# The order of work on the last tiles of a linear-attention block: statistics, masks, residual sums and transposes

## The chip, the cores and the metric

The kernel runs on one core of a Trainium2 chip. The metric is the device time of one execution in microseconds. Before the change the median of three runs is 949.95 us (949.16 to 952.21). One further execution, with the hardware profiler on, took 948.85 us; its span from the first to the last instruction is 947.1 us, and all times of single instructions below are counted from the start of that span.

The engines are PE (matrix products and transposes; PEld is its weight load), DVE (vector), ACT (scalar), POOL (GpSimd) and SP, whose queue issues every transfer of this kernel. Each works through its own list of instructions in order; the lists meet only at semaphores.

## The reference

Two pre-norm layers on x of 8 x 1024 tokens and 512 channels, in float32:

```
x = x + attn(layernorm(x))
x = x + ffn(layernorm(x))

attn(x):  q, k, v = split(x @ W_attn + b_attn)        # 16 heads of 32
          q, k = elu(q) + 1, elu(k) + 1
          for each token t:  kv += k_t v_t^T;  ksum += k_t       # causal
                             y_t = (q_t kv) / (q_t ksum + 1e-6)
          return y @ W_proj + b_proj
ffn(x):   x8 = clip(x, -448, 448).astype(float8_e4m3)
          w8 = clip(w, -448, 448).astype(float8_e4m3)
          return x8 @ w8.T + bias
```

## The kernel before

The 8192 tokens are 64 tiles of 128 (`NT` = 64), eight tiles to a sequence. Every engine has one hand-written loop over `n`, and the order of the calls in that loop is the order of its instructions. In pass `n` the loops work on several tiles at once:

- **PE** (L433 to L470): `ahead` (parts of the q, k, v projection of later tiles; in passes 59 to 62 only the v part of tile n+1, twelve 128x512 matmuls), `t_y(n-1)` (passes 61 on: y of the tile before is transposed on PE, four 128x128), `values(n)` (64 small matmuls: masked scores and state times v), `proj(n-1)` (twelve 128x512 matmuls; y and W_proj stand as high and low float16 halves, so matmuls 0 to 7 need the transposed high half `s_yth`, and 8 to 11 the low half `s_ytl`), `update(n+1)` (the tile's k-v products), `scores(n+1)`, and `ffn(n-2)` (four 128x512).
- **DVE** (L981 to L1022): `ahead` (here `v_out(n+1)`, two operations at L728), `t_y(n-1)` (low half of the transposed y, L779), `values(n)` (division; the result is `y`), `proj(n-1)` (residual sum of the attention, L786), `ln2(n-1)` (second layernorm's statistics, L700 to L705), `update(n+1)` (`mid` and `state`, L751 and L754), `scores(n+1)` (the causal masks, two operations at L739) and `ffn(n-2)` (the last residual sum of a tile, L844, which signals `s_res`).
- **ACT** (L655 to L693): in passes 61 to 63 `t_y(n-1)` (high half of the transposed y, L610), `ffn(n-3)` (the FFN's result from PSUM, `o16`); in passes 60 to 63 `t2(n-2)` (the normed row to float8 and to bfloat16, `x2b`), `k_tokens(n+1)` (`ktok`, which `update` on PE reads), `queries(n+1)`, and `spread(n+1)` (state and mid into the operand of `values`).
- **POOL** (L1159 to L1189): `k_split(n+2)`, `proj(n-1)` (inverse square root at L1029 and the norm at L1031, which gives `x2`), `spread(n+1)` (a part of mid, `s_near`, at L1052), `add_bf(n-1)` (L1095).
- **SP** (L1265 to L1298), in pass n: transpose `x2t` of tile n-2 (L1234, read by PE's `ffn(n-2)`), transpose of the k bytes of tile n+2 (L1222), then the store of tile n-2. In the code the pass ends so:

```
t2(n - 2)
t_k(n + 2)
sp.wait_ge(s_res, m + 1)            # m = n - 2
e.dma_start(out_d[m * P:(m + 1) * P, :], xs[:, m % NX, :])
```

So `x2t` of tile m+1 is issued behind the store of tile m, and that store waits for `s_res` of tile m, the residual sum of DVE's `ffn(m)`. This part is in both kernels the same. `tail(n)` is true from tile 60 on: from there y goes through PE's transposes and not through a transfer, and `update` and `scores` of the next tile stand ahead of `ffn` on PE. PSUM banks are taken in turn from a ring of four (`take`).

From pass 60 on DVE's `ffn(58)` stands at the end of pass 60, `ffn(59)` of 61, `ffn(60)` of 62, and `ffn(61)`, `ffn(62)` and the last tile's in pass 64. On PE, pass 63 is `t_y(62)`, `proj(62)` matmuls 0 to 3, `values(63)`, `proj(62)` 4 to 11, `t_y(63)`; pass 64 projects tile 63 in two halves of 256 columns (`last_proj`), then `ffn(61)`, the transposes of tiles 62 and 63, and their FFN.

Of the kernel before, what the change touches and what calls it, by code (L numbers as in the profile page):

```python
# [21 lines left out]
NT = B * T // P  # L22
# [28 lines left out]
def tail(n):  # L51
    return n >= NT - 4
# [31 lines left out]
def build(nc, x_d, wa_d, ba_d, wp_d, bp_d, wf_d, bf_d, out_d):  # L84
    ctx = ExitStack()
    with ctx:
# [133 lines left out]
        def _(e):  # L220
# [3 lines left out]
            def take(key, freed, value):  # L224

                r = ring["n"] % NR
                ring["n"] += 1
                if ring["free"][r]:
                    pe.wait_ge(*ring["free"][r])
                ring["free"][r] = (freed, value)  # L230
                bank[key] = R[r]
                return R[r]
# [4 lines left out]
            def transposes(out, ins):  # L237
                for i, a in enumerate(ins):
                    last = e.transpose(out[:, i * P:(i + 1) * P], a, ident[:, :])  # L239
                return last  # L240
# [112 lines left out]
            def t_y(n):  # L353
                out = take(("ty", n), s_ytl, n - NT + 5)
                pe.wait_ge(s_y, n + 1)
                transposes(out, [y[:, h * P:(h + 1) * P] for h in range(4)]).then_inc(s_ty, 1)

            def proj(n, first=0, end=12):
                out = take(("proj", n), s_x1, n + 1) if first == 0 else bank["proj", n]
                pe.wait_ge(s_wpl, 1)  # L360
                if tail(n):
                    pe.wait_ge(s_yth, n - NT + 5)
                else:
                    pe.wait_ge(s_yt[n % 2], 16 * (n // 2 + 1))
                mms = [(a + h, b, h) for a, b in ((0, wph), (0, wpl), (4, wph)) for h in range(4)]
                for i, (k, b, h) in list(enumerate(mms))[first:end]:
                    if tail(n) and i == 8:
                        pe.wait_ge(s_ytl, n - NT + 5)
                    mm = matmul(out[:, :], yt[:, n % 2, k, :], b[:, h, :], i == 0, i == 11)
                if end == 12:  # L370
                    mm.then_inc(s_proj, 1)
# [61 lines left out]
            for n in range(NT + 2):  # L433
                if n < NT:
                    if not tail(n):
                        scores(n)
                    ahead(chunks(n)[0])
                    if tail(n - 1):
                        t_y(n - 1)
                    if n:  # L440
                        ahead(chunks(n)[1])
                    if n == NT - 1:

                        proj(n - 1, 0, 4)
                    values(n)
                    if n == 0:
                        ahead(chunks(n)[1])
                if n == NT - 1:
                    proj(n - 1, 4, 12)
                    t_y(n)  # L450
                elif n == NT:
                    last_proj()
                elif 1 <= n < NT:
                    proj(n - 1)
                if n + 1 < NT and tail(n + 1):

                    update(n + 1)
                    scores(n + 1)
                if n == NT:
                    ffn(n - 3)  # L460
                    t2(n - 2)
                    pe.wait_ge(s_y, NT)
                    warm(8)
                    last_t2()
                    ffn(n - 2)
                    last_ffn()
                elif 2 <= n < NT - 1:
                    ffn(n - 2)
                if n + 1 < NT and not tail(n + 1):
                    update(n + 1)  # L470
# [225 lines left out]
        def _(e):  # L696
# [35 lines left out]
            def scores(n):  # L732
                dve.wait_ge(s_score, n + 1)
                dve.wait_ge(s_causal, 3)
                if n:
                    dve.wait_ge(s_av, n)
                for a in range(2):
                    dst = sm[half_rows(a), :, a, :].rearrange("p h (g t) -> p h g t", g=4)
                    made = e.tensor_tensor(dst, scored(a), causal_over(a), ALU.mult)  # L739
                made.then_inc(s_smd, 1)  # L740
# [36 lines left out]
            def t_y(n):  # L777
                dve.wait_ge(s_yth, n - NT + 5)
                e.tensor_tensor(yt[:, n % 2, 4:8, :], four(bank["ty", n][:, :]), yt[:, n % 2, 0:4, :],  # L779
                                ALU.subtract).then_inc(s_ytl, 1)  # L780
# [200 lines left out]
            for n in range(NT + 2):  # L981
                if n < NT:
                    if not tail(n):
                        scores(n)
                    if n + 8 < NT:
                        ln1(n + 8)
                    if n == 0:
                        proj_weight()
                    if n == 1:
                        ffn_sum(0, 2)  # L990
                    ahead(chunks(n)[0])
                    if tail(n - 1):
                        t_y(n - 1)
                    if n:
                        ahead(chunks(n)[1])
                    values(n)
                    if n == 0:
                        ffn_high()
                        ffn_round()
                        ahead(chunks(n)[1])  # L1000
                if 1 <= n < NT:
                    proj(n - 1)
                if n == NT - 1:
                    t_y(n)
                if 1 <= n < NT:
                    ln2(n - 1)
                if n == NT:
                    last_proj()
                if n + 1 < NT:
                    update(n + 1)  # L1010
                    if tail(n + 1):
                        scores(n + 1)
                if n == 1:
                    ffn_sum(2, 4)
                if n == NT:
                    last_norm()
                    ffn(n - 3)
                    last_t2()
                    ffn(n - 2)
                    last_ffn()  # L1020
                elif 2 <= n < NT - 1:
                    ffn(n - 2)  # L1022

        @block.gpsimd
        def _(e):
# [16 lines left out]
            def spread(n):  # L1042

                v = v1[:, n % NV, :, :, :].rearrange("p a (g h) w -> p a g h w", g=4)
                pool.wait_ge(s_pair, 3)
                pool.wait_ge(s_one, 2)
                if n >= NV:
                    pool.wait_ge(s_av, n - NV + 1)
                pool.wait_ge(s_mid, n + 1)
                held = mid[0:HALF, :].rearrange("p (g w) -> p g w", g=4).unsqueeze(2).broadcast_to([HALF, 4, 2, W])  # L1050
                rows = pair[:, :].unsqueeze(1).unsqueeze(3).broadcast_to([HALF, 4, 2, W])
                e.tensor_tensor(v[0:HALF, 1, :, 0:2, :], held, rows, ALU.mult).then_inc(s_near, 1)  # L1052
# [19 lines left out]
            def add_bp(m):  # L1072
                x = xs[:, m % NX, :]
                pool.wait_ge(s_xn, m + 1)
                pool.wait_ge(s_bias, 32)
                e.tensor_tensor(x, x, bp[:, :], ALU.add).then_inc(s_xb, 1)  # L1076
# [8 lines left out]
            def proj(n):  # L1085
                x = xs[:, n % NX, :]
                pool.wait_ge(s_var2, n + 1)
                if n >= 2:
                    pool.wait_ge(s_x28, n - 1)
                norm(x2[:, n % 2, :], x, st2[:, n % 4, :], s_rs2, s_x2, n)  # L1090
# [68 lines left out]
            for n in range(NT + 1):  # L1159
                if n < NT:  # L1160
                    if n + 8 < NT:
                        ln1(n + 8)
                    if n == 0:
                        values(n)
                    elif n + 8 < NT:
                        add_bp(n + 8)

                    if n % 4 == 3 and n + 8 < NT:
                        ln1_parts(n + 8)
                    if n + 2 < NT:  # L1170
                        k_split(n + 2)
                    if n % 4 < 3 and n + 8 < NT:
                        ln1_parts(n + 8)
                    if n:
                        values(n)
                    if 1 <= n < 8:
                        add_bp(n)
                if n == NT:
                    last_norm()
                    last_ffn()  # L1180
                elif n >= 1:
                    proj(n - 1)
                if n + 1 < NT:
                    spread(n + 1)
                if n == 0:
                    add_bp(n + 8)
                    add_bp(n)
                if 1 <= n < NT:
                    add_bf(n - 1)  # L1189
# [134 lines left out]
```

## Time and profile before

| | before |
|---|---|
| median of the runs | 949.95 us |
| profiled execution | 948.85 us |
| its span | 947.1 us |
| PE busy | 918.2 us, 97% of the span |
| DVE / ACT / POOL busy | 731.8 / 745.6 / 641.3 us |
| transfers issued by SP | 251840 packets, 96.25 MB |

A timeline row gives the start, the length, the engine, the line, the operation with its output and inputs, the shapes and the count; in brackets the idle time of the engine just before it and what ended it. Matmuls are pipelined and their ends are modelled, so a row of PE may be longer than the distance to the next one. A few matmul records are missing from a trace: a row `x3` of `wft,x2t` is an FFN of four.

### The profile page before, as it was taken

How to read it: one execution, taken by the hardware profiler on the slowest of the kernel's cores; microseconds unless marked ns; L12 is line 12 of the kernel's file. 1: busy time of each engine (PE TensorE's matmuls, PEld its weight loads, DVE VectorE, ACT ScalarE, POOL GpSimd, SP SyncE). 2: the span in 40 equal slices, each digit the busy share in tenths (PEclk: the TensorE clock that was granted, in tenths of full speed). 3: DMA queues.
4: the chain of work that ended last, by engine and by line, in shares of the span. 5: the costliest groups of instructions: out<-in, count | busy, mean ns of one | idle time of the engine just before them, and what ended most of it. 6: DMA issues, size and time to landing. Idle time of an engine off the chain costs nothing.

```text
span 947.1 us, 44776 instructions
## 1 busy us (share of the span) xinstructions
PE 918.2 (97%) x19470; PEld 490.5 (52%) x19532; DVE 731.8 (77%) x1404; ACT 745.6 (79%) x1358; POOL 641.3 (68%) x713
## 2 busy tenths in 40 slices
PE   5998999999999999999999999999999999999896
PEld 2455555555555555555555555555555555555454
DVE  6999879787777777778687687777778687676687
ACT  5788787877869688787877868788787878868874
POOL 5659877766767677676776667677676676764433
PEclk9999999999999999999999999999999999999999
DMA  8926564565464554565555465555555455462421
GB/s 268 143 41 109 109 119 103 97 119 97 95 122 100 98 116 104 96 114 105 95 114 107 91 116 106 89 118 108 92 114 112 89 114 110 90 103 59 76 69 59
DMA packets 252036, 99.12 MB, mean 105 GB/s; under 512 B 232384, under 2 KB 232640, under 8 KB 251840
## 3 DMA queue, kind: packets, MB, share of 16 engines
q1 hardware_dynamic: 251840, 96.25, 52.3%
q8 instruction: 154, 2.52, 1.1%
q14 instruction: 42, 0.34, 0.1%
HBM read 22.81 MB, written 16.78 MB: 42 GB/s over the span
## 4 chain that ended last, share of the span: by engine, by line
PE 90%; POOL 3%; issue 2%; ACT 2%; DVE 2%; SPq 1%; DMA 1%; ACTq 0%; POOLq 0%
PE R L235 77%; PE S L235 13%; POOL st L1029 1%; POOL xn L1031 1%; DMA x2t<-x2b 0%; ACT raw L477 0%; POOL xs L1076 0%; PE R L239 0%; DVE raw L739 0%; POOL raw L1062 0%; DMA xs<-in_L_attn_x 0%; ACT ktok L477 0%; SPq L1227 0%; DVE v L728 0%; ACT o L477 0%
## 5 line engine op out<-in xcount | busy, mean ns | idle before, releaser
L235 PE MATMUL R<-xt,wh 128*128 128x512 f16 x1024 | 306.2, 381 | 2.4 <-ACT wh L477 2.4
L716 DVE SCALAR_TENSOR_TENSOR qk<-qk,rel 128x512 f32<-128x512 f32 x128 | 112.8, 884 | 118.1 <-ACT rel L489 118.1
L477 ACT ACTIVATE raw<-qk 64x512 f32<-64x512 f32 x256 | 160.8, 628 | 48.9 <-PE S L235 45.7
L235 PE MATMUL R<-xt,wl 128*128 128x512 f16 x512 | 194.0, 380 | 0.0
L1083 POOL TENSOR_TENSOR yhl<-y,yhl 128x512 f16<-128x512 f32 x60 | 70.0, 1167 | 146.1 <-ACT yhl L477 146.1
L235 PE MATMUL R<-wh,xt 128*128 128x512 f16 x512 | 158.0, 379 | 0.0
L235 PEld LDWEIGHTS R<-xt,wh 128*128 128x128 f16 x1024 | 96.7, 98 | 116.0 <-DVE xt L882 2.6
L739 DVE TENSOR_TENSOR raw<-S,causal 64x1024 f32<-64x1024 f32 x128 | 155.9, 1218 | 0.9
L1029 POOL TENSOR_TENSOR st<-st,half 128x1 f32<-128x1 f32 x127 | 92.7, 730 | 90.6 <-DVE st L705 89.8
L235 PE MATMUL R<-wph,yt 128*128 128x512 f16 (+1 forms) x520 | 132.4, 377 | 3.9 <-ACT yt L477 1.9
L486 ACT ACTIVATE qk<-R,bqk,wm 128x512 f32<-128x512 f32 x128 | 98.9, 773 | 35.6 <-PE R L235 35.0
L728 DVE SCALAR_TENSOR_TENSOR v<-R,wm,bv 64x512 f32<-64x512 f32 x128 | 96.0, 750 | 8.2 <-PE R L235 5.7
L1062 POOL COPY raw<-qk 128x512 int16<-128x512 int16 x126 | 86.8, 717 | 21.2 <-DVE qk L716 14.9
L489 ACT ACTIVATE rel<-R,bqk,wm 128x512 f32<-128x512 f32 x128 | 98.5, 769 | 3.0 <-DVE qk L716 3.0
L235 PE MATMUL R<-wl,xt 128*128 128x512 f16 x256 | 97.0, 379 | 0.0
L700 DVE BATCH_NORM_STATS2 st<-xs 128x6 f32<-128x512 f32 x127 | 88.2, 694 | 6.4 <-DMA xs<-in_L_attn_x 2.5
L235 PEld LDWEIGHTS S<-v,raw 128*32 128x32 f32 x8192 | 76.2, 108 | 29.3 <-issue 27.1
L477 ACT ACTIVATE ktok<-raw 128x512 int16<-128x512 int16 x126 | 88.2, 771 | 0.1
L1076 POOL TENSOR_TENSOR xs<-xs,bp 128x512 f32<-128x512 f32 x64 | 84.6, 1322 | 4.6
L235 PE MATMUL S<-v,raw 128*32 128x33 f32 x8192 | 83.5, 198 | 2.5 <-issue 1.9
L1069 POOL TENSOR_TENSOR xnhl<-xn,xnhl 128x512 f16<-128x512 f32 x60 | 69.6, 1161 | 23.7 <-ACT xnhl L477 23.7
L477 ACT ACTIVATE v<-state 32x132 f32<-32x132 f32 x256 | 79.9, 312 | 3.8
(108 smaller groups left out, 1364.8 us busy)
## 6 DMA issues: line engine op xcount, KB each, us to landing
xs<-in_L_attn_x SPq DMA_DIRECT2D x64, 256.0 KB, 3.1
out<-xs SPq DMA_DIRECT2D x63, 256.0 KB, 2.4
raw<-in_L_attn_W_attn SPq DMA_DIRECT2D x3, 1024.0 KB, 9.5
xs<-in_L_attn_W_proj SPq DMA_DIRECT2D x4, 256.0 KB
raw<-in_L_ffn_weight SPq DMA_DIRECT2D x1, 1024.0 KB, 17.0
raw<-raw SPq DMA_TRANSPOSE x63, 3.7
x2t<-x2b SPq DMA_TRANSPOSE x62, 2.5
xt<-xnhl SPq DMA_TRANSPOSE x60, 3.5
```

What stands on the lines that cost most here:

```text
L235: return e.matmul(out, a, b, start=start, stop=stop, skip_group_check=True)
L477: return e.activation(out, in_, ACT.Copy, **more)
L486: e.activation(dst[:, i, :], bank["qkv", j, i][:, :], ACT.Exp, scale=UN[i // 4], bias=bqk[:, i:i + 1])
L489: e.activation(rel[:, u % 2, :], bank["qkv", j, i][:, :], ACT.Relu, scale=UN[i // 4], bias=bqk[:, i:i + 1]).then_inc(s_relu, 1)
L700: e.bn_stats(row[:, 0:6], src).then_inc(s_bn, 1)
L716: e.scalar_tensor_tensor(qk[j % 2][:, i, :], qk[j % 2][:, i, :], 1.0, rel[:, (u - 1) % 2, :], ALU.min, ALU.add).then_inc(s_phi, 1)
L728: made = e.scalar_tensor_tensor(v1[rows, n % NV, a, :, 0:32], heads(bank["qkv", j, 8 + t][rows, :]), UN_V[rows], heads(bv[rows, :]), ALU.m ...
L739: made = e.tensor_tensor(dst, scored(a), causal_over(a), ALU.mult)
L1029: e.tensor_tensor(row[:, 10:11], row[:, 9:10], half[:, :], ALU.pow).then_inc(s_rs, 1)
L1062: made = e.tensor_copy(khl[:, n % 2, w, :].rearrange("p (g t) -> p g t", g=4), words[:, w, :, :])
L1076: e.tensor_tensor(x, x, bp[:, :], ALU.add).then_inc(s_xb, 1)
L1083: e.tensor_tensor(yhl[:, n % 2, 1, :], y[:, :], yhl[:, n % 2, 0, :], ALU.subtract).then_inc(s_yl, 1)
```

## The change

Only the order of calls in four loops changes, for the passes 59 to 64; no operation is added or taken away, and SP's and ACT's lists stay as they are.

- **DVE**, passes 59 to 62: `update(n+1)` and the masks stand ahead of `ln2(n-1)`. `ffn` of a tile from 58 on comes later: `ffn(58)` at the end of pass 61, not 60; `ffn(59)` of pass 62, not 61; `ffn(60)` in pass 63 between the residual sum of tile 62 and `t_y(63)`. Pass 60 has no `ffn`.
- **POOL**, passes 59 to 62: `spread(n+1)` ahead of `proj(n-1)`.
- **PE**: `ffn(60)` moves from the end of pass 62 to pass 63, between `t_y(62)` and `values(63)`; `proj(62)` runs whole behind `values(63)`, with `t_y(63)` between its matmuls 0 to 7 and 8 to 11.

```
 PE     if n == NT - 1:
-           proj(n - 1, 0, 4)
+           ffn(n - 3)
        values(n)
    if n == NT - 1:
-       proj(n - 1, 4, 12)
+       proj(n - 1, 0, 8)
        t_y(n)
+       proj(n - 1, 8, 12)
...
-   elif 2 <= n < NT - 1:
+   elif 2 <= n < NT - 2:
        ffn(n - 2)
 DVE    if n == NT - 1:
+           ffn(n - 3)
            t_y(n)
+       if n + 1 < NT and tail(n + 1):
+           update(n + 1)
+           scores(n + 1)
        if 1 <= n < NT:
            ln2(n - 1)
...
-       if n + 1 < NT:
+       if n + 1 < NT and not tail(n + 1):
            update(n + 1)
-           if tail(n + 1):
-               scores(n + 1)
...
-       elif 2 <= n < NT - 1:
+       elif n < NT - 1 and tail(n - 1):
+           ffn(n - 3)
+       elif n >= 2 and not tail(n):
            ffn(n - 2)
 POOL
+       if n + 1 < NT and tail(n + 1):
+           spread(n + 1)
...
            proj(n - 1)
-       if n + 1 < NT:
+       if n + 1 < NT and not tail(n + 1):
            spread(n + 1)
```

DVE's list in pass 61 before, from the residual sum of tile 60 (`xs<-R1`) over its statistics (`st2`), `mid` and `state` of tile 62 and its masks (`raw`) to the last residual sum of tile 59 (`xs<-o16`), the v of tile 63 and the low half of y of tile 61 (`yt`):

```order
L786 SCALAR_TENSOR_TENSOR xs<-R1,wm,xs 128x512
L700 BN_STATS st2<-xs 128x6
L702 BN_AGGR st2<-st2 128x2
L704 TENSOR_SCALAR st2<-st2 128x1
L705 TENSOR_SCALAR st2<-st2 128x1
L751 TENSOR_TENSOR mid<-R2,state 128x132
L754 TENSOR_TENSOR state<-R3,mid 128x132
L739 TENSOR_TENSOR raw<-S,causal 64x4x256 x2
L844 TENSOR_TENSOR xs<-o16,xs 128x512
L728 SCALAR_TENSOR_TENSOR v1<-R1,wm,bv 64x16x32 x2
L779 TENSOR_TENSOR yt<-R2,yt 128x512
```

The statistics stand four operations earlier here than in the changed list, in which the sum is that of tile 58 (line numbers are one higher):

```order
L787 SCALAR_TENSOR_TENSOR xs<-R1,wm,xs 128x512
L752 TENSOR_TENSOR mid<-R2,state 128x132
L755 TENSOR_TENSOR state<-R3,mid 128x132
L740 TENSOR_TENSOR raw<-S,causal 64x4x256 x2
L701 BN_STATS st2<-xs 128x6
L703 BN_AGGR st2<-st2 128x2
L705 TENSOR_SCALAR st2<-st2 128x1
L706 TENSOR_SCALAR st2<-st2 128x1
L845 TENSOR_TENSOR xs<-o16,xs 128x512
L729 SCALAR_TENSOR_TENSOR v1<-R1,wm,bv 64x16x32 x2
L780 TENSOR_TENSOR yt<-R2,yt 128x512
```

The masks moved ahead of the statistics, and the row `xs<-o16` stays in its place but belongs to a tile one older.

PE's list from behind the scores of tile 63 to the projection of tile 62, as one piece of the difference (`wft,x2t` is the FFN of tile 60, `ident,y` the transposes of y of tile 62 and then 63, `wph` and `wpl` the projection of tile 62, `v1,raw` the values of tile 63):

```order
-L235 MATMUL R1<-wft,x2t 128x512 x4
-L239 MATMUL R2<-ident,y 128x128 x4
-L235 MATMUL R3<-wph,yt 128x512 x4
-L235 MATMUL S<-v1,raw 32x33 x64
+L239 MATMUL R1<-ident,y 128x128 x4
+L235 MATMUL R2<-wft,x2t 128x512 x4
+L235 MATMUL S<-v1,raw 32x33 x64
+L235 MATMUL R3<-wph,yt 128x512 x4
 L235 MATMUL R3<-wpl,yt 128x512 x4
-L235 MATMUL R3<-wph,yt 128x512 x4
 L239 MATMUL R0<-ident,y 128x128 x4
+L235 MATMUL R3<-wph,yt 128x512 x4
```

The FFN of tile 60 moved behind the transposes and stays ahead of the values; four matmuls of the projection moved behind the values, and its last four behind the transposes of tile 63.

## Rows read from the trace of the kernel before

**Rows 1.** Page, part 4: the chain that ended last, shares by engine

```profile
PE 90%; POOL 3%; issue 2%; ACT 2%; DVE 2%; SPq 1%; DMA 1%; ACTq 0%; POOLq 0%
```

**Rows 2.** Timeline of PE in passes 60 to 63

```profile
903.61 0.76 PE L235 MATMUL R<-v,ktok 64*32 64x33 f32 x64
...
913.45 1.04 PE L235 MATMUL R<-wph,yt 128*128 128x512 f16 x4 [1.12 <-DVE yt L779]
...
915.11 0.91 PE L235 MATMUL S<-qk 32*64 32x64 f32 x64
916.18 0.81 PE L235 MATMUL R<-wft,x2t 128*128 128x512 bf16 x3 [0.16 <-issue]
916.83 0.38 PE L235 MATMUL R<-wh,xt 128*128 128x512 f16 x1
...
922.34 0.60 PE L235 MATMUL R<-wph,yt 128*128 128x512 f16 x2 [0.56 <-issue]
...
924.19 1.04 PE L235 MATMUL R<-wph,yt 128*128 128x512 f16 x4 [0.38 <-DVE yt L779]
...
927.26 0.60 PE L239 MATMUL R<-ident,y 128*128 128x128 f32 x4
929.04 1.02 PE L235 MATMUL R<-wph,yt 128*128 128x512 f16 x4 [1.18 <-ACT yt L477]
929.99 1.30 PE L235 MATMUL S<-v,raw 128*32 128x33 f32 x128
```

**Rows 3.** Timeline of SP's queue: stores (L1298) and transposes of x2 (L1234)

```profile
901.56 0.33 SPq L1298 DMA_DIRECT2D out<-xs  x1
901.98 1.38 SPq L1234 DMA_TRANSPOSE x2t<-x2b  x1
...
911.15 0.33 SPq L1298 DMA_DIRECT2D out<-xs  x1
911.73 1.19 SPq L1234 DMA_TRANSPOSE x2t<-x2b  x1
```

**Rows 4.** Timeline of ACT in pass 60: x2b of tile 58, k of tile 61

```profile
898.80 0.63 ACT L477 ACTIVATE x2b<-x 128x512 bf16<-128x512 fp8e4 x1
899.34 1.43 ACT L477 ACTIVATE ktok<-raw 128x512 int16<-128x512 int16 x2
```

**Rows 5.** Timeline of DVE: statistics, masks, last residual sums, low half of y

```profile
895.41 0.69 DVE L700 BATCH_NORM_STATS2 st<-xs 128x6 f32<-128x512 f32 x1
...
897.08 2.45 DVE L739 TENSOR_TENSOR raw<-S,causal 64x1024 f32<-64x1024 f32 x2
899.55 1.98 DVE L844 TENSOR_TENSOR xs<-o,xs 128x512 f32<-128x512 f16 x1
...
910.42 0.70 DVE L844 TENSOR_TENSOR xs<-o,xs 128x512 f32<-128x512 f16 x1 [1.31 <-ACT o L477]
...
934.75 0.69 DVE L779 TENSOR_TENSOR yt<-R,yt 128x512 f16<-128x512 f32 x1 [0.84 <-ACT yt L477]
```

**Rows 6.** Waits of SP's queue, 880 to 947 us: in total, times, longest

```profile
SPq L1298 <- DVE xs L844: 36.8, 7, 8.0
```

**Rows 7.** Tile x2t, 880 to 947 us: time from issue to landing

```profile
DMA to landing us min/median/max: 2.4/2.7/2.9
```

**Rows 8.** Timeline of POOL in pass 59: the norm of tile 58

```profile
896.65 0.55 POOL L1029 TENSOR_TENSOR st<-st,half 128x1 f32<-128x1 f32 x1 [0.19 <-DVE st L705]
897.30 0.77 POOL L1031 TENSOR_SCALAR x<-xs,st 128x512 f32<-128x512 f32 x1
```

**Rows 9.** Windows at the end: busy us (count) by engine, then granted clock, DMA

```profile
943.50:945.40 1.90, 0.00 (x0) 0.00 (x0) 1.11 (x3) 0.11 (x1) 0.67 (x1) 0.98 0.45 164
945.40:947.10 1.70, 0.00 (x0) 0.00 (x0) 0.00 (x0) 0.00 (x0) 0.00 (x0) 0.50 0.38 125
```

**Rows 10.** Timeline of PE: the first 128x512 matmuls of the kernel

```profile
16.13 3.57 PE L235 MATMUL R<-xt,wh 128*128 128x512 f16 x8 [2.37 <-ACT wh L477]
19.49 1.45 PE L235 MATMUL R<-xt,wl 128*128 128x512 f16 x4
```

## The prediction

> **What bounds the kernel now.** I read the chain of work that ended last first: PE carries 90% of the span [rows 1]. So a change in the last passes counts only by what PE waits for there and by the chain from the last tile's y to the last store. The timeline of PE is next. Up to pass 59 the change leaves everything alone; in passes 61 to 63 PE stands still four times [rows 2]: 1.12 us for the low half of y of tile 60, 0.56 us with no releaser shown, 0.38 us for the low half of tile 61 and 1.18 us for the high half of tile 62, together 3.24 us. These are what a new order could win.
>
> The view that decides, I think, is another one, the timeline of SP's queue. It does not alternate freely: a store of a finished tile, then, 0.4 to 0.6 us behind it, the transpose `x2t` of the next tile [rows 3]. The row of pass 60 shows that the transpose waits for the store and not for its own data: ACT had written `x2b` of tile 58 at 898.80 + 0.63 = 899.43 [rows 4], yet its transpose was issued at 901.98, 0.42 us behind the store of tile 57 at 901.56 [rows 3], and that store went out 0.03 us after DVE's residual sum of tile 57 ended, at 899.55 + 1.98 = 901.53 [rows 5]. The queue's own waits say it in sum: stores waited for the residual sum seven times in the last 67 us, 36.8 us together [rows 6]. So the residual sum of tile m holds the transpose of tile m+1, and that transpose feeds PE's FFN of tile m+1. Before, this costs nothing: the store of tile 58 goes at 911.15, the transpose of tile 59 at 911.73 [rows 3], it lands 2.7 us later [rows 7], at 914.4, and PE comes to that FFN only at 916.18 [rows 2], 1.8 us later.
>
> **The change part by part.**
>
> *Masks ahead of statistics, `near` ahead of the norm.* DVE's statistics of tile 58 began at 895.41 and were with POOL at 896.65 [rows 5, 8], so 1.2 us; now they begin behind the masks (2.45 us, rows 5) and the state, about 3.3 us later than before. The norm on POOL (896.65 to 898.07, rows 8) and ACT's `t2` go with them, and ACT is in order: its k of tile 61, ready at 899.34 + 1.43 = 900.77 [rows 4], is ready at 904.1. PE began to use it at 903.61 [rows 2]: a new wait of 0.5 us. In return `values` gets its masks somewhat sooner, which is cover only, since PE comes to `values(60)` no earlier. In passes 60 to 62 ACT had more room and I take 0.
>
> *Residual sums later.* In pass 61 DVE no longer waits 1.31 us for ACT's FFN copy [rows 5] ahead of `v_out` and the low half of y, so PE's 1.12 us go [rows 2]. With the 0.5 us of above, and the few tenths by which PE's rows overlap, the scores of tile 62 end at 915.1 in place of 915.11 + 0.91 = 916.0: -0.9 us.
>
> But the sum of tile 58 now stands at the end of pass 61, behind masks of tile 62 and statistics of tile 60. From the end of those scores: 0.1 + masks 2.45 + statistics 1.2 + sum 0.70 [rows 5] = 4.45 us, so 919.55. Then the store, 0.42 us on the queue, the transpose of tile 59 at 920.0, landing 2.7 us later [rows 3, 7]: 922.7. PE's next work, unchanged, is exactly the FFN of tile 59. **It waits 915.1 to 922.7, 7.6 us**, and starts 6.6 us later than at 916.18. Queued behind it on PE are v of tile 63 and all the rest, so nothing else fills the hole.
>
> The same once more for tile 60. Before, PE needed from 916.18 to 927.86 (929.04 less 1.18, rows 2) for that FFN, v of tile 63, the transposes of tile 61, values, projection, update and scores, the FFN of tile 60 and the transposes of tile 62: 11.7 us, less the 0.56 and 0.38 us that should not return, less 0.87 us for the FFN of tile 60: 9.9 us. So PE is ready for the FFN of tile 60 at 922.7 + 9.9 = 932.6, the scores of tile 63 having ended 0.5 us before. DVE then does the masks of tile 63, the statistics of tile 61 and only then the sum of tile 59: 932.1 + 4.45 = 936.5; store and transpose 0.4 us, landing 2.7 us: 939.6. **PE waits 7.0 us**, because this FFN was put ahead of `values(63)`; before, it was behind nothing late. `values(63)` starts at 939.6 + 0.9 = 940.5 and not at 929.99: +10.5 us.
>
> *PE's transposes of tile 63 inside the projection of tile 62.* These save the 1.18 us wait (already in the sum) and let y of tile 63 go out as soon as it is there. But the last four matmuls of tile 62 now end later, so its residual sum on DVE too, and behind that stand the sum of tile 60 and then the low half of tile 63, on which the last projection waits. From the start of `values(63)`: `values` up to 1.30, eight matmuls at 0.22, four transposes up to 0.60, four matmuls up to 1.04 [rows 2], 4.7 us less the overlap of the rows, 4.6 us; then three DVE operations of 0.7 us each (0.70 and 0.69, rows 5) = 6.7 us. Before it was 934.75 + 0.69 - 929.99 = 5.45 us. So **+1.3 us** on the final chain; from there on (statistics, norm, transposes, FFN, store) the order is the same, and the late transpose of tile 61 (behind the sum of tile 60) lands beside DVE's work on tile 63.
>
> Sum: 10.5 + 1.3 = **+11.8 us**. For the profiled execution that is 948.85 + 11.8 = 960.65; against the median, which lies 1.1 us higher, 949.95 + 11.8 = 961.75.
>
> *The clock after a stall.* Two holes of 7 us in PE are something the trace of before does not have in the middle. At its end it has one: PE was idle from 943.5 on, and from about 945.4 the granted clock is 0.50, the 1.2 GHz level [rows 9]. And its start shows what work costs at that level (the matmuls of the start follow 2.37 us of idle): eight 128x512 in 16.13 to 19.49, 0.42 us each, four more in up to 1.45 us [rows 10], against 0.22 us each later (three in 916.18 to 916.83, rows 2); the twelve cost up to 2.2 us too much before the pace doubled, 2.0 us if the last row's overlap is left out. So a price per restart between 0 (the clock stays) and 3.4 us (I allow half as much again and more, as one start says little of the spread); I take 2.0 us for the first restart, where 12 matmuls of that shape follow, and 1.7 us for the second, where `values` with its small matmuls may not be slowed: +3.7 us.
>
> The Trainium skill says in TensorE: Matmul & The Clock Gate, Part 1, that "the default state is throttled, and activity releases the throttle", and in its section Why this matters for your kernels that idle gaps between bursts of matmuls bring half clock back. By that rule both restarts are slow (965.4 us); without it the sum stays at 961.7 us. The end of the trace agrees with it (0.50 two microseconds after the last matmul), and no row shows a long hole in the middle.
>
> Forecast: 949.95 + 11.8 + 3.7 = **965.4 us**, slower by 1.6%.
>
> **The rivals.**
>
> *Stalls without the clock's part.* The holes come, and PE returns at 2.4 GHz. For: the trace has no restart in the middle, and where DVE is late anyway a slow PE is hidden. Against it the fall at the end [rows 9], after a shorter hole. 961.7 us; down to 960.5 if the masks or the landing are quicker than I take them (2.4 us is the fastest landing, rows 7).
>
> *One hole only.* If ACT or DVE slip so that the second transpose meets a PE that is late anyway, only the first hole and the tail count: 949.95 - 0.9 + 7.6 - 1.3 + 1.3 = 956.7. Against: after the first hole PE, DVE and SP stand in the same order to one another as before it.
>
> *The other side: not slower, the change does what it says.* It needs the transposes not to be held by the stores, that is SP going past a store that waits. Then the 3.24 us of waits go, 0.5 us come for k, 1.3 us for the tail, and about 1 us because PE comes to `values(63)` before its masks are done: 949.95 - 0.4 = 949.5, within 0.3%. It decides from the point where the transpose of tile 59 lands before 915.1, that is where its store goes out before 912. Against it: the 2.55 us that a ready `x2b` of tile 58 stood behind a store [rows 3, 4]. If in addition none of these new waits came, it would be 946.7 us.
>
> **How the numbers follow.** Forecast (both holes, slow restarts) 0.64; both holes without the clock 0.24; one hole 0.04, and 0.01 for something much slower; no hole, 949.5 us, 0.05; all gains, 946.7 us, 0.02. About 0.3%, 2.85 us, is what a measurement of this kernel can tell from no change. Slower by more than that: 0.64 + 0.24 + 0.04 + 0.01 = 0.93; within: 0.05; faster: 0.02. The range: from 960.5 (no clock cost, quick landing) to 968.5 (961.7 and 3.4 us at each restart).
>
> **What would show it.** In the profile after: a store of tile 58 near 919.6 and the transpose of tile 59 at once behind it; PE's first `wft,x2t` row of pass 61 with some 7.6 us idle before it and a transfer of `x2t` as releaser; the same once more, near 7 us, ahead of the FFN of tile 60; matmuls 128x512 about 0.42 us apart behind each hole and a granted clock under 1 there; ahead of the update of tile 61 a wait of some 0.5 us for ACT; no more 1.12 us ahead of the low half of tile 60's projection; 1 to 1.5 us of idle ahead of the last group of `last_proj`. The prediction is wrong if the stores of tiles 58 and 59 go out as early as before, or if PE's holes are there but the end is not later by their sum.

## The result and the profile after

The changed kernel takes 966.32 us in the median of four runs (966.21 to 966.43), against 950.70 us for the kernel before in the same rounds: ratio 1.0163, 95% interval 1.015 to 1.0175. The forecast was 965.4 us with a range of 960.5 to 968.5, so the time lies 0.9 us above the forecast and inside the range. The forecast counted from 949.95 us; by what the change adds, 15.5 us were forecast and 15.6 us came.

| | before | after |
|---|---|---|
| median of the runs | 950.70 us | 966.32 us |
| profiled execution | 948.85 us | 966.43 us |
| its span | 947.1 us | 964.7 us |
| PE busy | 918.2 us | 922.0 us |

The chain of work that ended last, shares by engine, in the page of the changed kernel (the row that answers to [rows 1]):

```profile
PE 86%; DVE 4%; POOL 3%; issue 2%; ACT 2%; DMA 1%; SPq 1%; POOLq 0%; DVEq 0%
```

PE has lost four points of the chain, DVE has gained two. PE's timeline of passes 60 to 63 shows where (the columns are those of [rows 2]):

```profile
897.19 0.76 PE L235 MATMUL R<-v,ktok 64*32 64x33 f32 x64
...
907.37 0.75 PE L235 MATMUL R<-v,ktok 64*32 64x33 f32 x64 [1.00 <-ACT ktok L478]
...
917.65 0.91 PE L235 MATMUL S<-qk 32*64 32x64 f32 x64
926.18 1.49 PE L235 MATMUL R<-wft,x2t 128*128 128x512 bf16 x3 [7.62 <-DMA x2t<-x2b]
...
936.24 0.91 PE L235 MATMUL S<-qk 32*64 32x64 f32 x64
937.08 0.66 PE L239 MATMUL R<-ident,y 128*128 128x128 f32 x4
944.81 1.49 PE L235 MATMUL R<-wft,x2t 128*128 128x512 bf16 x3 [7.07 <-DMA x2t<-x2b]
946.23 1.69 PE L235 MATMUL S<-v,raw 128*32 128x33 f32 x128
...
953.10 1.05 PE L235 MATMUL R<-wph,yt 128*128 128x256 f16 x8 [1.17 <-DVE yt L780]
```

The two holes are there, ahead of the FFN of tile 59 and ahead of that of tile 60, both ended by a transpose of x2: 7.62 and 7.07 us by these rows. But a row `x3` lacks the record of one matmul, and the FFN's weight loads show that it is the first one:

```profile
925.77 0.13 PEld L235 LDWEIGHTS R<-wft,x2t 128*128 128x128 bf16 x2 [7.35 <-DMA x2t<-x2b]
...
944.40 0.13 PEld L235 LDWEIGHTS R<-wft,x2t 128*128 128x128 bf16 x2 [6.90 <-DMA x2t<-x2b]
```

So PE stood still from 917.65 + 0.91 = 918.56 to 925.77 and from 937.08 + 0.66 = 937.74 to 944.40: 7.2 and 6.7 us. The waits of 1.12 us for the low half of tile 60 and of 1.18 us for the high half of tile 62 [rows 2] are gone. A wait of 1.00 us for k of tile 61 has come, and one of 1.17 us in the last projection.

SP's queue tells what held the transposes (stores are L1306, transposes of x2 L1242), beside ACT's writing of k of tile 61 and of `x2b` of tile 59:

```profile
905.86 1.20 SPq L1242 DMA_TRANSPOSE x2t<-x2b  x1
...
922.88 0.34 SPq L1306 DMA_DIRECT2D out<-xs  x1
923.31 1.23 SPq L1242 DMA_TRANSPOSE x2t<-x2b  x1
...
941.46 0.34 SPq L1306 DMA_DIRECT2D out<-xs  x1
941.89 1.22 SPq L1242 DMA_TRANSPOSE x2t<-x2b  x1
```

```profile
905.74 1.38 ACT L478 ACTIVATE ktok<-raw 128x512 int16<-128x512 int16 x2
...
914.90 0.63 ACT L478 ACTIVATE x2b<-x 128x512 bf16<-128x512 fp8e4 x1
```

`x2b` of tile 59 was written at 914.90 + 0.63 = 915.53, and its transpose was issued at 923.31, 7.8 us later and 0.43 us behind the store of tile 58. DVE's timeline shows what that store waited for, the residual sum (L845) behind the masks (L740) and the statistics (L701), and further down the sum of tile 60 ahead of the low half of y of tile 63 (L780):

```profile
902.55 0.68 DVE L845 TENSOR_TENSOR xs<-o,xs 128x512 f32<-128x512 f16 x1
...
918.60 2.46 DVE L740 TENSOR_TENSOR raw<-S,causal 64x1024 f32<-64x1024 f32 x2 [0.21 <-PE S L235]
921.09 0.69 DVE L701 BATCH_NORM_STATS2 st<-xs 128x6 f32<-128x512 f32 x1
...
922.17 0.68 DVE L845 TENSOR_TENSOR xs<-o,xs 128x512 f32<-128x512 f16 x1
...
951.76 0.68 DVE L845 TENSOR_TENSOR xs<-o,xs 128x512 f32<-128x512 f16 x1
952.36 0.69 DVE L780 TENSOR_TENSOR yt<-R,yt 128x512 f16<-128x512 f32 x1
```

The sum ends at 922.85, the store goes at 922.88. In the queue's own waits over the last stretch (880 to 964 us; in total, times, longest) the 36.8 us of [rows 6] have become 52.8 us:

```profile
SPq L1306 <- DVE xs L845: 52.8, 7, 15.6
```

The granted clock is the number ahead of the last two in a row of this view of windows (busy us and count for PE, PEld, DVE, ACT and POOL stand before it):

```profile
917.00:926.00 9.00, 1.56 (x128) 1.51 (x130) 5.40 (x10) 4.23 (x10) 3.57 (x4) 0.66 0.18 49
926.00:928.00 2.00, 1.82 (x5) 0.72 (x5) 0.00 (x0) 0.00 (x0) 0.00 (x0) 0.50 0.65 125
928.00:930.00 2.00, 2.00 (x6) 0.64 (x5) 0.00 (x0) 0.00 (x0) 0.00 (x0) 0.50 0.00 0
930.00:932.00 2.00, 2.00 (x18) 1.11 (x20) 0.40 (x1) 0.00 (x0) 0.00 (x0) 0.96 0.00 0
...
940.00:944.00 4.00, 0.00 (x0) 0.00 (x0) 2.06 (x6) 0.84 (x2) 2.90 (x3) 0.55 0.35 98
944.00:946.00 2.00, 1.19 (x3) 0.43 (x4) 0.00 (x0) 0.00 (x0) 0.06 (x1) 0.50 0.04 8
```

PE stood idle, its clock fell to 0.50 (1.2 GHz) within each hole, and the work behind each hole began at that level.

As a ledger along PE (before from [rows 2]; the update of tile 60 from the same timeline, where it begins at 894.51; the FFN of tile 59 by its weight loads, which begin at 915.95 before):

| point | before | after | later by |
|---|---|---|---|
| update of tile 60 begins | 894.51 | 897.19 | 2.68 |
| scores of tile 62 end | 916.02 | 918.56 | 2.54 |
| FFN of tile 59 begins | 915.95 | 925.77 | 9.82 |
| values of tile 63 begin | 929.99 | 946.23 | 16.24 |
| end of the span | 947.1 | 964.7 | 17.6 |

The first 2.68 us arise ahead of everything that the change moves: they come mostly from a stop in pass 59 that both kernels have and from the clock behind it (last section). What is left, 17.6 - 2.68 = 14.9 us, is the change's by these two profiles; the medians of the runs differ by 15.6 us.

### The profile page after: what moved, and what is told of

It reads as the page before. It is cut to its first block, busy times and chain, and to the rows that moved or that the text cites. A ratio compares the mean times of both kernels' runs of the same rounds, so it can differ in the third digit from the quotient of the medians.

```text
span 964.7 us, 44775 instructions
## 1 busy us (share of the span) xinstructions
PE 922.0 (96%) x19470; PEld 492.2 (51%) x19532; DVE 729.5 (76%) x1404; ACT 745.8 (77%) x1358; POOL 642.7 (67%) x713
## 4 chain that ended last, share of the span: by engine, by line
PE 86%; DVE 4%; POOL 3%; issue 2%; ACT 2%; DMA 1%; SPq 1%; POOLq 0%; DVEq 0%
PE R L235 73%; PE S L235 13%; DMA x2t<-x2b 1%; POOL st L1035 1%; DVE raw L740 1%; DVE wl L890 1%; POOL xn L1037 1%; DVE st L701 1%; DVE qk L717 1%; POOL xs L1082 0%; DVE xs L845 0%; PE R L239 0%; POOL raw L1068 0%; ACT wh L478 0%; DMA xs<-in_L_attn_x 0%
## 5 line engine op out<-in xcount | busy, mean ns | idle before, releaser
L740 DVE TENSOR_TENSOR raw<-S,causal 64x1024 f32<-64x1024 f32 x128 | 155.9, 1218 | 1.9 <-PE S L235 0.9
L487 ACT ACTIVATE qk<-R,bqk,wm 128x512 f32<-128x512 f32 x128 | 98.9, 772 | 34.9 <-PE R L235 34.3
L729 DVE SCALAR_TENSOR_TENSOR v<-R,wm,bv 64x512 f32<-64x512 f32 x128 | 96.0, 750 | 17.8 <-PE R L235 15.3
L701 DVE BATCH_NORM_STATS2 st<-xs 128x6 f32<-128x512 f32 x127 | 88.2, 694 | 6.1 <-DMA xs<-in_L_attn_x 2.2
L787 DVE SCALAR_TENSOR_TENSOR xs<-R,wm,xs 128x512 f32<-128x512 f32 x63 | 47.3, 751 | 52.0 <-PE R L235 52.0
```

The lines of the kernel that those rows point to most:

```text
L487: e.activation(dst[:, i, :], bank["qkv", j, i][:, :], ACT.Exp, scale=UN[i // 4], bias=bqk[:, i:i + 1])
L701: e.bn_stats(row[:, 0:6], src).then_inc(s_bn, 1)
L729: made = e.scalar_tensor_tensor(v1[rows, n % NV, a, :, 0:32], heads(bank["qkv", j, 8 + t][rows, :]), UN_V[rows], heads(bv[rows, :]), ALU.m ...
```

## The experiments

The theory: the residual sum of tile m, put late on DVE, holds the store of tile m on SP, and this store holds the transpose of tile m+1, for which PE waits twice; 1.2 GHz behind each wait is the rest. The rivals: the new places of masks and statistics, or PE's new order, make the holes; or SP's order has no part in it and the transposes' data is late.

**Take away the queue's order.** `e1_store_behind` is the changed kernel with the store of a tile one tile later from pass 60 on, so that it stands behind the next transpose.

```
 SP, behind t2(n - 2) and t_k(n + 2)
-    elif n >= 2:
-        m = n - 2
+    elif n >= 2 and n != NT - 4:
+        m = n - 2 if n < NT - 4 else n - 3
         sp.wait_ge(s_res, m + 1)
         e.dma_start(out_d[m * P:(m + 1) * P, :], xs[:, m % NX, :])
...
+    if n == NT + 1: store of tile n - 3
```

> The changed kernel with one thing undone elsewhere: from pass 60 on SP issues the store of a tile behind the next tile's transpose of x2 and behind the k transpose, no longer ahead of them; the late residual sums on DVE stay. Theory (the queue): the transposes of tiles 59 and 60 go out near 912 and 922 us, PE's two holes of 7.6 and 7.1 us and both slow restarts are gone, the rest of the change stays: 949 to 951 us, 0 to 1 us under the kernel before. Rival (the late residual sums and statistics cost by themselves, through DVE, POOL and ACT): at least 958 us, with PE still waiting several us ahead of the FFN of tiles 59 and 60 for something other than a transfer.

Measured: 951.37 us (median of 10 runs; before 950.75 in the same rounds), ratio 1.0001, interval 0.999 to 1.0013. (The ratios come from the comparison of all runs and are not the quotients of the two medians.) That is 0.4 us above the range expected, and no gain against the kernel before can be seen. SP's transposes of tiles 59 and 60 and then PE's FFN of these tiles:

```profile
914.89 1.19 SPq L1242 DMA_TRANSPOSE x2t<-x2b  x1
...
924.87 1.20 SPq L1242 DMA_TRANSPOSE x2t<-x2b  x1
```

```profile
917.83 1.04 PE L235 MATMUL R<-wft,x2t 128*128 128x512 bf16 x4
...
928.65 1.03 PE L235 MATMUL R<-wft,x2t 128*128 128x512 bf16 x4
```

Neither row of PE has a wait in brackets. DVE's sum of tile 58 is as late as in the changed kernel, only nothing hangs on it. 966.32 - 951.37 = 15.0 us come back by SP's order alone, so the data of the transposes was not late, and the masks and PE's order make no hole by themselves.

**One part of the change alone.** `e2_sums_only` is the kernel before with DVE's residual sums at the later places and nothing else.

```
 DVE    if n == NT - 1:
+           ffn(n - 3)
            t_y(n)
...
-   elif 2 <= n < NT - 1:
+   elif n < NT - 1 and tail(n - 1):
+       ffn(n - 3)
+   elif n >= 2 and not tail(n):
        ffn(n - 2)
```

> The kernel before with one part of the change alone: DVE's residual sums of tiles 58 to 60 one pass later; masks, statistics, POOL and PE as before. Theory (the queue): both holes are there, near 7.6 and 7.9 us, with the clock at its lower level behind each: 965 to 968 us. Rival (the masks ahead of the statistics are the cause, through the late norm): 949 to 952 us, as the kernel before.

Measured: 966.33 us (4 runs), ratio 1.0158, interval 1.0135 to 1.018. Store and transpose on SP, then PE's FFN of tiles 59 and 60:

```profile
922.08 0.34 SPq L1301 DMA_DIRECT2D out<-xs  x1
922.50 1.23 SPq L1237 DMA_TRANSPOSE x2t<-x2b  x1
```

```profile
925.01 1.89 PE L235 MATMUL R<-wft,x2t 128*128 128x512 bf16 x4 [7.23 <-DMA x2t<-x2b]
...
943.43 1.89 PE L235 MATMUL R<-wft,x2t 128*128 128x512 bf16 x4 [7.58 <-DMA x2t<-x2b]
```

Here all four matmuls are in the rows. The sums alone make both holes and the whole loss. The other parts neither add to it nor take from it by more than a measurement can tell.

**The other parts without the sums.** `e3_sums_back` is the changed kernel with the sums at the places of before (the diff of e2, turned round).

> The changed kernel with the residual sums of tiles 58 to 60 put back to where they stood before; all else of the change stays. Theory (the queue): no hole over 3 us; what is left is the wait for k of tile 61 (0.5 to 1.0 us), waits of about 2.4 us each for the low half of y of tiles 60 and 61 and the later end: 3.3 us over the kernel before, 953 to 955 us. Rival (masks ahead of statistics are the cause): 962 us or more.

Measured: 951.27 us (10 runs), ratio 1.0003, interval 0.9989 to 1.0016. That the loss goes was right; the 2 to 4 us that were to stay were not there. They were put down to the low half of y in passes 61 and 62. PE waited for it 1.11 and 0.53 us, against 1.12 and 0.38 us in the kernel before [rows 2]:

```profile
915.16 1.04 PE L235 MATMUL R<-wph,yt 128*128 128x512 f16 x4 [1.11 <-DVE yt L780]
...
925.90 1.04 PE L235 MATMUL R<-wph,yt 128*128 128x512 f16 x4 [0.53 <-DVE yt L780]
```

DVE's row of the sum ahead of that low half shows why:

```profile
912.14 0.69 DVE L845 TENSOR_TENSOR xs<-o,xs 128x512 f32<-128x512 f16 x1 [1.41 <-ACT o L478]
```

The sum waited for ACT's copy of the FFN, 1.41 us, as it did before (1.31, [rows 5]). Masks ahead of statistics change the order within DVE's list ahead of that wait, not what ends it.

**Masks and PE's order each alone.** `e5_masks_only` is the kernel before with masks ahead of statistics on DVE and `spread` ahead of the norm on POOL; `e6_pe_only` is the kernel before with PE's new order. Their diffs are the corresponding parts of the diff of the change.

> The kernel before with masks ahead of statistics on DVE and the near part ahead of the norm on POOL, nothing else. Theory: ktok of tile 61 is late by about 1.0 us as in the changed kernel (1.00 us there), no hole of 7 us since the residual sums stand where they were; the high half of tile 62 is still waited for, about 1.2 us. In sum 0.5 to 1.5 us above the kernel before: 951.3 to 952.3 us, within 0.3%. Rival (the masks' place is what makes the sums late, and so the holes): 8 us or more above.

> The kernel before with PE's order of the change only (the FFN of tile 60 ahead of the values of tile 63, the projection of tile 62 behind them with the transposes of tile 63 inside). Theory: the transpose of x2 of tile 60 is there before its FFN, no hole of 7 us; the 1.18 us ahead of the projection of tile 62 goes, and PE comes to the values of tile 63 before their masks are done: 1 to 2 us of wait in its place. In sum 0 to 1 us above the kernel before: 950.8 to 951.8 us, within 0.3%. Rival (the early FFN is a part of the loss by itself): a hole of 3 us or more ahead of it and 954 us or more.

Measured: 951.04 us, ratio 1.0003 (0.9992 to 1.0014), and 951.65 us, ratio 1.0008 (0.9992 to 1.0024); before in these rounds 950.95 us. On PE, in e5 the update of tile 61 and in e6 the values of tile 63:

```profile
905.77 0.75 PE L235 MATMUL R<-v,ktok 64*32 64x33 f32 x64 [1.08 <-ACT ktok L477]
```

```profile
930.74 1.72 PE L235 MATMUL S<-v,raw 128*32 128x33 f32 x128 [1.99 <-DVE raw L740]
```

The masks' part costs a wait for k, as in the changed kernel. PE's order trades the 1.18 us ahead of the projection of tile 62 for 1.99 us ahead of the values of tile 63. Both stay within what can be told from no change (e5 lies 0.3 us under the range expected for it, e6 inside its own), and neither has a hole of several us.

**Take away the clock's part.** `e4_fill` is the changed kernel with needless matmuls in the two holes; they write the FFN's own bank, which the FFN then overwrites, so the output is the same.

```
 PE, ffn(n), ahead of the wait for x2t
+   for _ in range({59: 28, 60: 26}.get(n, 0)):
+       matmul(out[:, :], wph[:, 0, 0:P], wph[:, 0, :], True, True)
```

> The changed kernel with 28 and 26 needless 128x512 matmuls ahead of PE's FFN of tiles 59 and 60, into the PSUM bank that the FFN then overwrites: about 6.0 and 5.6 us of work inside the two holes; the result is the same. Theory (half the clock behind each hole is a price of its own): the granted clock stays 1.00 through passes 61 to 63, the 128x512 matmuls behind the holes are 0.22 us apart, and the time is 2.5 to 4 us under that of the changed kernel: 962.5 to 964 us. Rival (the slow restart is hidden behind DVE): the time stays at 966.3 us within 0.7 us.

Measured: 962.57 us (4 runs), ratio 1.0117, interval 1.0102 to 1.0133. The window of the first hole and PE's rows:

```profile
917.00:926.00 9.00, 7.93 (x158) 4.14 (x151) 5.28 (x10) 4.13 (x10) 3.58 (x4) 1.00 0.20 53
```

```profile
925.67 1.04 PE L235 MATMUL R<-wft,x2t 128*128 128x512 bf16 x4 [1.07 <-DMA x2t<-x2b]
...
933.99 0.91 PE L235 MATMUL S<-qk 32*64 32x64 f32 x64
...
942.16 1.04 PE L235 MATMUL R<-wft,x2t 128*128 128x512 bf16 x4 [1.05 <-DMA x2t<-x2b]
...
944.35 1.04 PE L235 MATMUL R<-wph,yt 128*128 128x512 f16 x4
```

The holes still end with the transfer (1.07 and 1.05 us after the last needless matmul), so the fillers delay nothing; only the clock differs, 1.00 where it was 0.66. It is worth 966.32 - 962.57 = 3.75 us.

**A version that keeps the gain.** `e7_mix` is the kernel before with the sums of tiles 58 and 59 one pass later, that of tile 60 behind the last tile's statistics, and SP's stores as in e1. `e8_sum60_last` puts the sum of tile 60 one place further, behind DVE's part of the last norm.

```
 SP as in e1
 DVE, end of the passes, as in e2
 DVE, pass 64
     last_proj()
+    ffn(n - 4)          # e7
...
     last_norm()
+    ffn(n - 4)          # e8
     ffn(n - 3)
```

> The kernel before with two changes only: DVE's residual sums of tiles 58 and 59 one pass later and that of tile 60 behind the last tile's statistics, and SP's stores from pass 60 on one tile later, behind the transpose of x2 and that of the k bytes. PE, POOL, the masks and the statistics stand as in the kernel before. Theory (the loss is the queue's order, and the gain of the change lies in the sums' places): no hole ahead of the FFN of tiles 59 and 60; the wait of 1.12 us ahead of the low half of tile 60's projection goes, and ktok keeps its early time, since the norm isn't moved: 1 to 2 us below the kernel before, 948.8 to 949.8 against 950.8 us. Rival (what the waits took comes back as other waits of DVE and ACT in passes 62 and 63): 950.8 us, within 0.3%. A third, that the late stores of tiles 60 to 62 add to the end: 1 to 2 us above, 951.8 to 952.8.

> e7_mix with one row moved: the residual sum of tile 60 stands behind DVE's part of the last norm, not between the last tile's statistics and that norm. In e7_mix POOL's inverse square root of the last tile took 0.99 us beside that sum, and the norm on DVE began 0.50 us late; in the kernel before that inverse square root took 0.55 us with nothing beside it. Theory (the sum beside POOL's inverse square root is what lengthens it): 0.55 us again, the last norm 0.4 to 0.9 us earlier, no new wait: 0.4 to 0.9 us below e7_mix, 947.9 to 948.4 us if e7_mix lies at 948.8. Rival (the 0.99 us has another cause, or the sums of tiles 60 and 61 together now hold the cast of the last x2t on DVE): 948.8 us as e7_mix, or up to 0.5 us above.

Measured: e7 948.82 us (12 runs; before 950.95), ratio 0.9989, interval 0.9978 to 1.0; e8 950.56 us (12 runs; before 950.96), ratio 0.9986, interval 0.9973 to 0.9998. Both are some 0.1% faster, less than what a measurement of this kernel can tell from no change. Up to the values of tile 63 PE does win: from the start of the update of tile 60 it takes 34.3 us in both profiles (896.19 to 930.46 and 895.41 to 929.73), 1.2 us less than before (35.5). From there to the end of the span it gives back 0.7 us in e7 and 1.0 us in e8 (17.8 and 18.1 us against 17.1). In e7 DVE's sum of tile 60 runs beside POOL's inverse square root of the last tile; the two rows:

```profile
939.74 0.90 DVE L844 TENSOR_TENSOR xs<-o,xs 128x512 f32<-128x512 f16 x1
940.05 0.99 POOL L1105 TENSOR_TENSOR st<-st,half 128x1 f32<-128x1 f32 x1
```

In e8, without the sum beside it, the same POOL operation takes 0.55 us, but PE's last FFN now waits for DVE's cast of the transposed x2, which stands behind the two sums:

```profile
939.29 0.55 POOL L1105 TENSOR_TENSOR st<-st,half 128x1 f32<-128x1 f32 x1
...
943.15 1.03 PE L235 MATMUL R<-wft,x2t 128*128 128x256 bf16 x8 [0.91 <-DVE x2t L828]
```

So by the profiles e8's theory of the 0.99 us held, and its rival (the cast held by two sums) took what this gave. The times do not decide between e7 and e8: e8's median lies outside both ranges expected for it (947.9 to 948.4 us, or up to 949.3 us), but the two ratios to the kernel before hardly differ. From the values of tile 63 on, neither of these two orders ends earlier than that of before.

## Why the prediction was right, step by step

**The mechanism** was right as it stands in the prediction: residual sum, store, transpose of the next tile, FFN. e1 breaks it at SP and e2 makes it from DVE alone. That SP does not pass a waiting store, the point on which the "other side" hung, is seen in the changed kernel's queue: 7.8 us in which a ready `x2b` stood behind a store.

**k of tile 61**: 0.5 us was forecast, 1.00 us came. The norm's shift of 3.3 us was nearly right (statistics 0.90 us after the start of the update of tile 60 before, at 895.41, and 4.28 us after it in the changed kernel, at 901.47), but the inverse square root on POOL then took 0.93 us and not the 0.55 of [rows 8]: the step left out that DVE's residual sum of tile 57 now runs just beside it. It also left out that PE began 0.25 us after ACT had written k (905.74 + 1.38 = 907.12, then 907.37).

**The start of hole 1**: -0.9 us was forecast, -0.14 us came (2.54 less 2.68). The wait of 1.00 us took the place of the 1.12 us that went, and the few tenths taken for PE's overlapping rows were no gain.

**The holes**: 7.6 and 7.0 us were forecast. PE's rows read 7.62 and 7.07 us, which is luck: with the matmul that has no record the holes are 7.2 and 6.7 us, some 0.4 us less than forecast each. In the first, the way from the scores' end to the end of the sum was taken at 4.45 us and was 4.29 us (918.56 to 922.85), and the landing was taken at 2.7 us, while PE began 2.46 us after the issue (923.31 to 925.77). The low clock is not seen in that start: it took 2.51 us in e2, behind a hole and at the low clock (922.50 to 925.01), and 2.48 us in e4 at full clock (923.19 to 925.67). PE's 9.9 us between them can be read from e1, where nothing of the clock disturbs it: 928.65 - 917.83 = 10.8 us, less a stop of 1.01 us that it has there, 9.8 us.

**The tail**: 1.3 us was forecast; PE waits 1.17 us for the low half of tile 63, behind the sum of tile 60 (rows of DVE, 951.76 and 952.36). From the start of the values of tile 63 to the end of the span it is 18.5 us against 17.1 us before, but a part of this is the slow clock: in e4 it is 18.1 us (943.12 to 961.2), so 1.0 us belongs to the order.

**The clock**: 3.7 us was forecast, 3.75 us came by the medians. By the profiles of the changed kernel and of e4 the first restart, from the FFN of tile 59 (925.77 and 925.67) to the scores of tile 63, took 10.47 against 8.32 us, so 2.15 us (forecast 2.0). The second, from the FFN of tile 60 (944.40 and 942.16) to the projection of tile 62 (947.85 in the timeline of the changed kernel), took 3.45 against 2.19 us, so 1.26 us (forecast 1.7); the values of tile 63, which the prediction thought might not be slowed, took 1.69 us there against 1.30 us in e4. The two profiles differ by 3.5 us of span, 3.4 of which these two terms make. The rule quoted from the Trainium skill, TensorE: Matmul & The Clock Gate, Part 1, by which both restarts are slow, agrees with the trace: 0.50 from 926 to 930 and from 944 to 946 us.

**The sum without the clock**: +11.8 us was forecast, and e4 lies 962.57 - 950.75 = 11.8 us above the kernel before; by the two profiles, from the start of the update of tile 60 to the end, it is 11.45 us (64.04 against 52.59). That is partly luck: the gain of 0.9 us that did not come (0.76 us too little) is made up by holes that are together some 0.7 us shorter than forecast and by a tail 0.3 us shorter.

**The rivals**: stalls without the clock's part is what e4 makes by hand (961.7 forecast, 962.57 measured), and the changed kernel is not it, since its clock fell. One hole only (956.7 us) did not come: after the first hole all lists stood to one another as before, and the second transpose was as late as the first: it was issued 4.74 us after the end of the scores ahead of it (937.15 to 941.89), the first 4.75 us (918.56 to 923.31). That rival's own sum takes off 1.3 us that the prediction derives from nothing; its 11.8 us less the second hole of 7.0 would have given 954.8 us.

## What to carry to other kernels

A queue that issues transfers in order is one more engine: before a step that signals a store is put later, look at what stands behind that store on its queue, and who waits for it. Where an operation must come late, move its store behind the loads and transposes that others need; here that alone was worth 15 us of 966. The two stalls of PE cost more here than their length, because the work behind them started at the low clock, and that part (3.75 us beside 13.9 us of holes) could be measured by filling the holes with needless matmuls. And before a wait is read off a row to a few tenths, look whether all of the row's records are there.

## What the runs showed that was not expected

**POOL beside a residual sum of DVE.** POOL's inverse square root on one column takes 0.55 us [rows 8], but in the changed kernel

```profile
902.71 0.93 POOL L1035 TENSOR_TENSOR st<-st,half 128x1 f32<-128x1 f32 x1 [3.66 <-DVE st L706]
```

It ends at 903.64, 0.41 us after DVE's sum (902.55 to 903.23) ends; in e7 it ends at 941.04, 0.40 us after a sum that ends at 940.64. e8 takes the sum away and has 0.55 us again. It looks as if POOL's operation waits within its own row until the sum is done. The kernel before seems to show the other side: DVE's sum of tile 57 took 1.98 us [rows 5] and not 0.70, where two POOL operations ran beside it until 900.99, 0.54 us before its end. The Trainium skill, SBUF — State Buffer, section SBUF: two separate sides, states that a DVE operation with two SBUF inputs and a GpSimd operation that reads SBUF share one pair of ports, and that the later one waits for the whole instruction of the other; this sum reads two tensors, and the rows agree.

**A stop of PE in pass 59 that no list explains.** In each profiled kernel PE breaks off the values of tile 59 after 103 of their 128 recorded matmuls for 1.86 to 2.41 us, with no releaser; in the changed kernel and in e3:

```profile
892.55 0.54 PE L235 MATMUL S<-v,raw 128*32 128x33 f32 x25 [2.14 <-issue]
```

```profile
892.22 0.40 PE L235 MATMUL S<-v,raw 128*32 128x33 f32 x25 [2.13 <-issue]
```

Stops of the same length have different ends: in the window behind them, 892 to 896.5 us,

```profile
892.00:896.50 4.50, 3.95 (x35) 0.62 0.32 62
```

the clock is 0.62 in the changed kernel (columns: PE's busy time and count, granted clock, DMA share, GB/s), and 1.00 in e3:

```profile
892.00:896.50 4.50, 4.28 (x147) 1.00 0.32 62
```

Of the ten profiled kernels four have a clock under 1 in that window (the changed kernel, e1 and e4 0.62, e2 0.74, behind stops of 2.13 to 2.41 us), and six have 1.00 (behind stops of 1.86 to 2.41 us). From the end of the stop to the update of tile 60 it is 4.64 us in the changed kernel (892.55 to 897.19) and 3.02 us in the kernel before (891.49 to 894.51): 1.6 of the 2.68 us that the profiled execution of the changed kernel had lost ahead of the change. 0.3 us more is the longer stop, and 0.8 us was there before it. The kernel before ranges over several us in its own runs (948.32 to 954.24 in one set of 29). That this stop is behind that whole range was not tested. In the window of it one transfer of instructions is recorded, which may be its cause; no run here tried that, and it stays open.
